# Cross-attention and a mixture of experts in one program: the block barrier between the two stages is taken out, and the expert stage's first steps are placed inside the last attention batch

## What is computed

```python
x = x + attention(layernorm(x), ctx, ctx, mask)      # 16 query heads of 32, 2 key/value heads, rope, softmax, then @ wo
xn = layernorm(x)
logits = xn @ Wr + expert_bias
top_v, top_i = top_k(logits, 2);  probs = softmax(top_v)
eo = (silu(xn @ Wg[e]) * (xn @ Wu[e])) @ Wd[e]       # 8 experts, inner width 256
out = sum over the two chosen experts of probs * eo
x = x + out + (silu(xn @ Sg) * (xn @ Su)) @ Sd       # the shared expert, inner width 512
```

## Time and profile before

| | us |
|---|---|
| median of 3 runs (1552.31 to 1552.96) | 1552.71 |
| the profiled execution | 1552.61 |
| its span, from the first to the last record | 1550.8 |
| PE busy | 1455.0 (94%) |
| ACT busy | 909.1 (59%) |
| DVE busy | 952.0 (61%) |
| POOL busy | 535.2 (35%) |
| last matmul of the attention block begins | 864.82 |
| first gate product of the expert block begins | 890.51 |

### The profile page before, as it was taken

One profiled execution on the slowest core, in us unless ns is written; L12 is line 12 of the kernel. 1 busy time (PEld: TensorE's weight loads), 2 busy tenths in 40 slices (PEclk: granted clock), 3 DMA queues, 4 the chain that ended last, 5 costly groups with the idle time before them and its releaser, 6 DMA issues. The chain is left out here.

```text
span 1550.8 us, 37262 instructions
## 1 busy us (share of the span) xinstructions
PE 1455.0 (94%) x11434; PEld 1179.7 (76%) x11434; DVE 952.0 (61%) x2637; ACT 909.1 (59%) x2052; POOL 535.2 (35%) x667
## 2 busy tenths in 40 slices
PE   6698999998999989999988599999999999999997
PEld 5587787887877878878767378787887888888885
DVE  4577777877777777787765366666664333333332
ACT  2588988877888878898896222222221344444442
POOL 2243231422423314224122052222224455546553
PEclk9799999999999999999999689999999999999999
DMA  4334344453453443534434602222225877886552
GB/s 155 96 105 141 111 137 138 114 156 103 131 166 106 139 134 114 167 109 123 126 107 130 218 35 83 83 93 87 92 73 164 231 196 158 233 226 118 110 88 36
DMA packets 141530, 198.94 MB, mean 128 GB/s; under 512 B 34951, under 2 KB 72591, under 8 KB 141330
## 3 DMA queue, kind: packets, MB, share of 16 engines
q1 hardware_dynamic: 118914, 156.23, 32.7%
q0 software_dynamic: 17952, 33.64, 11.3%
q10 hardware_dynamic: 4464, 6.55, 1.3%
HBM read 97.10 MB, written 69.35 MB: 107 GB/s over the span
## 5 line engine op out<-in xcount | busy, mean ns | idle before, releaser
L877 DVE CUSTOM_DVE_ANT_0 a_probs<-a_psum,a_bias 128x512 f32<-128x512 f32 x512 | 348.6, 686 | 175.0 <-PE a_psum L713 166.6
L527 ACT ACTIVATE a_probs<-a_probs,a_low 128x512 f32<-128x512 f32 x512 | 368.6, 720 | 107.7 <-DVE a_low L877 103.5
L625 PE MATMUL a_psum<-a_ident,a_probs 128*128 128x128 f32 x2048 | 318.9, 279 | 20.4 <-DVE a_xT_lo L834 5.5
L625 PEld LDWEIGHTS a_psum<-a_ident,a_probs 128*128 128x128 f32 x2048 | 243.3, 142 | 92.5 <-issue 38.8
L713 PE MATMUL a_psum<-a_kT,a_q_stack 128*128 128x512 f32 x512 | 249.8, 489 | 9.2 <-issue 5.6
L533 ACT ACTIVATE a_probsT<-a_psum 128x512 f32<-128x512 f32 x400 | 233.8, 584 | 13.3 <-issue 6.6
L1221 POOL DMA_INDIRECT out<-b_y,b_pairs_sb x71 | 113.2, 1594 | 151.2 <-DMA out<-b_y,b_pairs_sb 83.6
L733 PE MATMUL a_psum<-a_probsT,a_v 128*32 128x128 f32 x4096 | 140.4, 278 | 8.8 <-ACT a_probsT L533 5.5
L457 POOL CAST a_w_hi<-a_w_raw 128x256 fp32r<-128x256 f32 x96 | 38.2, 398 | 303.4 <-DMA a_w_raw<-in_L_ffn_Wd 129.6
L1664 DVE SCALAR_TENSOR_TENSOR b_v_hidden<-b_v_hidden,b_psum 128x256 f32<-128x256 f32 x71 | 29.9, 421 | 163.7 <-ACT b_v_hidden L1323 93.9
L733 PEld LDWEIGHTS a_psum<-a_probsT,a_v 128*32 128x32 f32 x4096 | 105.5, 110 | 31.6 <-issue 17.9
(11 more groups left out here) (206 smaller groups left out, 3157.3 us busy)
## 6 DMA issues: line engine op xcount, KB each, us to landing
b_w<-w_halves SPq DMA_DIRECT2D x16, 1536.0 KB
a_q_stack<-a_qT_hi SPq DMA_DIRECT2D x256, 64.0 KB, 2.0
a_q_stack<-a_qT_lo SPq DMA_DIRECT2D x256, 64.0 KB, 2.0
w_halves<-a_w_hi SPq DMA_DIRECT2D x96, 128.0 KB, 1.8
w_halves<-a_w_lo SPq DMA_DIRECT2D x96, 128.0 KB, 1.8
a_x_in<-in_x SPq DMA_DIRECT2D x32, 256.0 KB, 3.0
a_ctx_in<-in_ctx SPq DMA_DIRECT2D x32, 256.0 KB, 3.6
a_x_res<-in_x SPq DMA_DIRECT2D x32, 256.0 KB, 3.0
```

The source lines that it names most:

```text
L527: nc.scalar.activation(probs[:, h % 2, t], probs[:, h % 2, t], ACT.Exp, bias=low[:, h % H, t:t + 1], scale=-1.0, accum_out=total[:, h // G ...
L625: last = nc.tensor.transpose(out[:, P * i:P * (i + 1)], src(i), identity[:])
L877: nc.vector.tensor_tensor_reduce(probs[:, h % 2, t], psum[:, t % 2], bias[:, t], 1.0, HUGE, ALU.add, ALU.min, low[:, h % H, t:t + 1]).then ...
```

## The change

Both stages now write into one block. `attention_phase` and `ffn_phase` return one function per engine; those of the experts are generators, and the attention's `body` calls `next(following)` at the places where a piece of the expert stream is to stand. What is left of it follows after "end". All buffers of the attention get a fixed address (`ATTENTION_PLACES`), so that the expert buffers laid over them are free when they are written. One psum tensor, one identity and one `half` serve both.

- **SP**, in batch 7 at head 1: loads of Sg and Su and of the router and tables (8 transfers; before, Sg and Su were issued by ACT). At the start of "end": the eight tiles of blocks 0 and 1, ahead of the residual loads. The waits for all stores of the attention come later, ahead of the first transfer that needs them.
- **POOL**, in batch 7: rounding and subtraction of Sg and the rounding of Su at heads 1 and 2, the subtraction of Su at head 9. In "end": three roots ahead of `output_low`, the fourth after it.
- **ACT**: after "end" the load of Sd, then the four copies and roundings of block 0, and no more rounding of Sg and Su.
- **DVE**: statistics of block 0's tiles 0 to 2 and two normalisations ahead of the last `scale`; the other steps of block 0 in turn with the four residual adds. No more subtraction of Sg and Su.
- **PE**: the transposes of tiles 0 and 1 ahead of the output products, those of tiles 2 and 3 between them. In "end" the output products use two psum banks in turn in place of four, so tile t waits for the add of tile t-2. The router product waits for the last add.

```diff
@@ attention, product_bank @@
-            return (PRODUCT, OUT, 0, 1)[t] if part == "start" else (PRODUCT, TURN, 0, 1)[t] if part == "end" else PRODUCT
+        return (PRODUCT, OUT, 0, 1)[t] if part == "start" else (PRODUCT, TURN)[t % 2] if part == "end" else PRODUCT
@@ attention, SP: body @@
                     if part == "end":
+                next(following)
                         for t in range(TT):
...
+                if h == 1 and part == "last":
+                    next(following)
...
-                for i in range(2):
-                    sp.wait_ge(stored[i], 16 + 16 * B * TT // 2)
-                sp.wait_ge(s["w_stored"], 32 * E * PIECES)
@@ attention, POOL: body @@
                     if part == "end":
+                next(following)
                         output_low(b, par, -1)
...
+                if part == "last" and h in (1, 2, 9):
+                    next(following)
                         if 0 <= h - PIECE_HEAD < PIECES:
                             split_piece(b, h - PIECE_HEAD)
@@ attention, PE: project_out and body @@
+                elif t >= 2:
+                    pe.wait_ge(s["x2_ready"], upto(b, "wo", t - 2))
...
                         for t in range(TT):
+                    if t < TT - 1:
+                        next(following)
                             for c in range(DC):
                                 project_out(part, b, par, t, c)
@@ experts, SP @@
+        sp.wait_ge(attention["xT_filled"], TILES)
+        sp.wait_ge(attention["ctxT_filled"], TILES)
+        sp.dma_start(raw[:, 0], sg.rearrange("(c p) n -> p c n", p=P)).then_inc(s["raw_in0"], 16)
+        sp.wait_ge(attention["q_filled"], TILES)
+        sp.wait_ge(attention["kv_filled"], TILES)
+        sp.wait_ge(attention["q_added"], TILES)
+        sp.dma_start(raw[:, 1], su.rearrange("(c p) n -> p c n", p=P)).then_inc(s["raw_in1"], 16)
...
+        yield
+        sp.wait_ge(attention["low_ready"], B * H * TT)
+        for j in range(2):
                 for t in range(TT):
-                    load_x(1, t)
+                load_x(j, t)
+        yield
@@ experts, POOL @@
+        pool.wait_ge(attention["kv_filled"], TILES)
                 nc.gpsimd.memset(router[:], 0.0).then_inc(s["constants_set"], 1)
-                pool.wait_ge(s["constants_set"], 1)
+        pool.wait_ge(attention["q_filled"], TILES)
+        round_weights(sg_hi, 0)
+        split_weights(sg_lo, sg_hi, 0)
+        yield
+        pool.wait_ge(attention["qT_filled"], HG * (B - 1))
+        round_weights(su_hi, 1)
+        yield
+        pool.wait_ge(attention["qT_filled"], HG * B)
+        split_weights(su_lo, su_hi, 1)
+        yield
@@ experts, ACT @@
+        act.wait_ge(attention["out_filled"], HG * B)
+        for j in range(GH):
+            act.wait_ge(attention["stacked"][j], 64 * HG * B)
                 load_raw(sd, 2)
...
+        for t in range(TT):
+            x_copy(t)
+            x_high(t)
@@ experts, PE @@
+        x_transposes(0)
+        x_transposes(1)
+        yield
+        x_transposes(2)
+        yield
+        x_transposes(3)
+        yield
+        pe.wait_ge(attention["x2_ready"], TILES)
                 pe.wait_ge(s["consts_ready"], 1)
                 votes(0)
```

2830 lines of the change are left out of this document (1426 added, 1404 removed).

## The result

| | before | changed |
|---|---|---|
| median, lowest and highest of 4 runs each | 1552.84 (1552.31 to 1553.70) | 1532.18 (1531.03 to 1533.83) |
| ratio, with its 95% interval | | 0.9874 (0.9857 to 0.9890) |
| the profiled execution's span | 1550.8 | 1529.5 |
| PE busy | 1455.0 (94%) | 1447.6 (95%) |

The forecast was 1532.0. The sum is right; several of its terms are not, and they cancel. One of the four executions of run 2 took 2603.25 us, with a granted clock of 0.786, and is left out of that run's median.

What follows compares the result with a forecast made beforehand. PE, 94% busy, was taken as the bound, with time lost where it stands still at the block boundary. Forecast: 1552.61 - 22.1 + 1.5 = 1532.0 us; range 1528.2 to 1536.5.

Steps and rivals of the forecast that it cites:

- The boundary is order, not data: Between attention and experts: almost the whole 25.30 us gap is order; router product ends 22.1 us earlier.
- `a_att` 0.3 us late, with a bound of 2 us: End of attention on DVE: block 0's statistics and normalisations delay `a_att` by 0.3 us, bounds nothing and 2 us.
- Rival 1: End of attention: the eight loads slow each other, output products start 2 us later, 1534.0 us; chance 0.10.
- The first 12 products left cold: First output tile on PE: 4.43 us at clock 0.61 kept, leaving in 1.6 us against 2.8 us.
- rival 3: Batch 7 loses nothing and transposes keep PE's clock up, first 12 output products take 2.8 us: 1528.9 us; chance 0.11.
- The round of the residual, 5.64 us from add to add, unchanged: Output's residual adds: store and load still take 5.64 us; as sign, the residual's load still releases the last add.
- 14.7 us behind the router product, no term: Router product to the end of DVE's normalisation held by the memset: the same 14.7 us expected, no term.
- Batch 7, +1.5 us with bounds 0 and 5: Sg and Su steps moved into batch 7 delay the chain of pieces: 1.5 us charged, bounds 0 and 5.
- rival 2: Batch 7: a stacking behind 2 MB in SP's queue makes ACT wait, 5 us in place of 1.5, 1535.5; chance 0.14.
- less what SP spends anyway on stackings between the pieces: Batch 7: only part of POOL's 3 to 5 us lateness arrives at the chain, reduced by SP's stacking time.
- The span behind the first block: Rest of the kernel after the first block: no change expected; a change over 1 us counts as wrong.
- the rule given for the range: Range of the total: from rival 3 to rival 2, each with 1 us for what the bounds leave.

Runs made afterwards that it cites:

- run 2: Changed kernel with the transposes of tiles 0 and 1 behind the first output tile's 12 products, not ahead; 1537.81 us (median of three), 0.9890 of the kernel before.
- Run 6: Run 5's kernel with all four tiles' transposes behind the 48 output products and the low parts on DVE behind the residual adds; 1540.37 us, 0.9902 of the kernel before.
- Run 5: Changed kernel with the eight loads of blocks 0 and 1 issued on SP ahead of the last weight piece's store; 1533.24 us, 0.9860 of the kernel before.
- the repetition: The changed kernel unaltered, profiled and timed again, also listed as 11; 1534.50 us, 0.9880 of the kernel before.
- run 1: Changed kernel with POOL's clearing of the gather rows written as eight memsets in place of one; 1536.16 us, 0.9877 of the kernel before.
- run 7: Run 5's kernel with Sd rounded earlier on ACT, and POOL's Sd subtraction and clearing of the gather rows moved earlier; 1530.66 us, 0.9842 of the kernel before.
- run 8: Run 5's kernel with nine first-tile products not waiting for POOL's last low part, and the router product waiting for three adds; 1529.65 us, 0.9845 of the kernel before.
- run 9: Runs 4, 5 and 8 together, Sd rounded earlier on ACT and subtracted on DVE, gather rows cleared in three parts; 1523.84 us, 0.9800 of the kernel before.
- run 10: Changed kernel with only block 0's tiles ahead of the last piece and POOL's Sg and Su steps between the pieces; 1531.24 us, 0.9858 of the kernel before.
- run 4: Changed kernel with POOL's Sg and Su steps ahead of the third, seventh and tenth piece of batch 7; 1530.70 us, 0.9847 of the kernel before.
- run 3: Changed kernel with the loads of Sg, Su, router and tables issued one head earlier in batch 7; 1535.74 us, 0.9872 of the kernel before.
- run 12: The kernel before, unaltered, profiled and timed again; 1557.36 us against 1555.20, ratio 1.0016.
- the third group: Runs 9 to 12, including the repetition, measured on one chip; the kernel before took 1549.8 to 1565.0 us there in 25 executions.

## Why the prediction was right, and where not

**The boundary is order, not data: right.** The router product ended 19.9 us earlier (890.58 against 870.65), and 24.4 us earlier counted from the end of `a_spread` (41.19 us before, 16.82 now; forecast 19.1). Run 6 splits it: 3.3 us for the place between the products, 1.6 for the clock of the first tile, the rest for what was loaded and prepared before. Run 5, with a cold first tile as forecast, has 2.83 + 15.55 = 18.4 us against the 19.1.

**`a_att` 0.3 us late, with a bound of 2 us: right in the first profile, too narrow a bound.** It was on time there, and 2.25 us late in the repetition. On time, because DVE's statistics and normalisations took 3.97 us from the end of its last copy (849.46 to 853.43) and not 4.65; the roots held neither normalisation (0.54 us each). The step took SP as free at 841.50 and the tiles as landing 3 us later. What sets this is the last piece in the same queue, which the prediction moved nowhere: loads behind a chained store inherit its lateness. Behind the store `a_att` was 1.7 to 3.6 us late in four of six traces; with the loads one place earlier, from run 5 on, it was on time in all six. Rival 1 had the effect and blamed the eight loads.

**The first 12 products left cold: not so in the first profile, colder still in the repetition (5.26 us).** I left 1.6 us in; the profile had 2.83 us (full clock), so that rival 3's half came true there. Rival 3's reason, that the transposes keep the clock up, doesn't suffice after run 5: the same instructions at the same distances gave 1.00 once and 0.67 the next time. The Trainium skill says in "TensorE: Matmul & The Clock Gate", section "Part 1: The HAM clock gate", that the intervals in which activity is judged run free of the kernel, so the same kernel shows different numbers of slow products from run to run. The rows of runs 1, 5 and 7 agree. Work in the gap goes with the full clock in the two traces that have it, runs 8 and 9: the nine products ran 0.23 us from one to the next. With two traces, and a full clock in three of the five that have the transposes and then a pause of 2.1 to 2.4 us (changed, 1 and 10, not 5 and 7), this is possible and not shown; what the filled gap gives for certain is the 2.4 us of idleness.

**The round of the residual, 5.64 us from add to add, unchanged: not what decided.** The sign that was named, a last add still released by the residual's load, didn't come. From the end of the second add to the start of the last it was 868.83 - 863.59 = 5.24 us, and PE ended last there, not the load. The round is a bound just behind PE's; it came to the front in runs 2, 6, 8, 9 and 10, where an add waits for `a_x_res`.

**14.7 us behind the router product, no term: right to 0.02 us.** The 14.72 us hide a shift that didn't matter: the gap subtraction was held 1.55 us longer. Run 7 shows that both holds are POOL's.

**Batch 7, +1.5 us with bounds 0 and 5: the mechanism right, the size wrong, and rival 2 partly right.** The pair of profiles has +2.8. Over all traces the eight with the loads and POOL's steps where the changed kernel has them (changed, 11, 1, 2, 5 to 8) had 85.4 to 88.0 us, mean 86.8; the two of the kernel before 83.4 and 81.5. So the price is 3 to 5 us, near rival 2's 5. ACT's waits for stackings show two shares of it.

The first is the one that the prediction charged for. The step that failed is "less what SP spends anyway on stackings between the pieces": the delay of the first piece, 5.2 us (784.87 against 779.68), less the 1.7 us by which the batch started late, is 3.5 us, and 2.6 of them arrived at ACT's wait (4.5 us for 1.9). Over the eight traces this wait is 3.9 us in the mean, against 1.9 and 1.4 in the kernel before, so it accounts for some 2.3 us. With POOL's steps between the pieces it is 0.2 us in run 4 and absent in runs 9 and 10.

The second is rival 2's cause. The four stackings issued behind Sg and Su landed 3.6 to 5.3 us after their issue in these eight traces, where the kernel before has 1.9 to 2.0 at this place. ACT waited for them in seven of the eight, not in the first profile: 0.8 to 2.7 us, 1.4 in the mean over all eight. Runs 4, 9 and 10 still have this wait (1.6, 1.6 and 2.6 us). Run 3, which has none, is one trace. What the prediction put at nothing beside the pieces is therefore a term of about 1.4 us. That the 2 MB and not the six small transfers issued with them slow the stackings is likely, but no run separates the two.

**The span behind the first block:** it changed by 1.4 us, where over 1 us was to count as wrong. Part of it may be the clock in the 14.4 us behind the normalisation: 0.87, where the kernel before has 0.81 (last column but two):

```profile
905.28:919.70 14.42, 14.16 (x56) 11.40 (x57) 10.96 (x32) 5.12 (x9) 2.69 (x4) 0.81 0.15 56
```

From block 1's transposes to the last record of a compute engine, run 12 had 1.3 us less than the first trace of the same kernel, so a difference of this size is within one kernel's scatter.

**What stays open.** The part ahead of batch 7 has the same instruction order in nearly all of these kernels, and took 765 to 775 us. The 1.7 us of the first row of the table of stretches are of this kind; no run asks where they come from, and the 1532.0 that was met so closely was met partly by luck: the medians of the changed kernel were 1532.18 in the first comparison and 1534.50 in the third group. By the rule given for the range its low end, 1 us below rival 3, would be 1527.9 and not 1528.2; that decides nothing here.
